# Values laid out feature by feature for the head mixing, and first-layer heads issued in pairs, in a two-layer gated transformer kernel on one core

## The reference, cut to what matters

```
# L0 attention: 16 heads of 64; ctx gives keys and values
q, k, v = query @ Wq.T, key @ Wk.T, value @ Wv.T       # 1024 columns = 16 heads x 64
weights = softmax(q @ k^T / 8 + padding mask + causal mask)   # per head, 256 x 256
out = (weights @ v) @ Wo.T + bo

# L0 feed-forward, first half: a small attention between the 16 heads of ONE token, HD = 16
q  = (h @ Wq + bq).reshape(b, t, H, HD)
kv = ((h @ Wdown + bdown) @ Wup + bup).reshape(b, t, H, 2 * HD)
k, v = split(kv, 2, axis=-1)
att = softmax(einsum('bthd,btgd->bthg', q, k) / 4)
out = einsum('bthg,btgd->bthd', att, v)
# ... then a mixture of 8 experts (We), gated per token
```

## Time and profile before

| what | value |
|---|---|
| median of three runs | 2798.7 us (2793.26 to 2803.64) |
| the profiled execution | 2801.4 us, its span 2799.6 us |
| busy over the span | PE 2515.2 us (90%), PEld 2056.0, DVE 1772.2 (63%), ACT 1268.1 (45%), POOL 958.5 (34%) |
| mean granted TensorE clock | 0.957 of full |
| first layer | from 0 to about 1490 us, 16 bodies with attention and two short ones behind |
| second layer | the rest, untouched by the change |

### The profile page before, as it was taken

How to read it: one execution, slowest core, us unless ns; L and a number is a source line. 1 busy time by engine, 2 the same in 40 slices (tenths; PEclk the granted TensorE clock), 3 DMA queues, 4 the chain that set the end, 5 groups by cost and what they waited for, 6 DMA issues and landing times. The chain is left out here.

```text
span 2799.6 us, 48038 instructions
## 1 busy us (share of the span) xinstructions
PE 2515.2 (90%) x16128; PEld 2056.0 (73%) x16128; DVE 1772.2 (63%) x3970; ACT 1268.1 (45%) x3939; POOL 958.5 (34%) x878
## 2 busy tenths in 40 slices
PE   6989999999999999999845699999999999999998
PEld 5767777777777777777635477777787777777877
DVE  3488888888788888888873544445444444444541
ACT  5644555445554456545402344444443433444441
POOL 1344544444444454443441223233222222232320
PEclk9999999999999999999956899999999999999999
DMA  4000000000000000000004000000000000000000
GB/s 138 13 5 16 13 4 15 15 15 12 4 15 15 15 12 4 15 15 8 5 4 153 8 9 13 15 15 15 15 15 15 15 15 4 11 15 15 15 8 8
DMA packets 25857, 51.67 MB, mean 18 GB/s; under 512 B 6272, under 2 KB 7040, under 8 KB 24640
## 3 DMA queue, kind: packets, MB, share of 16 engines
q1 hardware_dynamic: 25792, 50.84, 5.5%
HBM read 42.44 MB, written 8.39 MB: 18 GB/s over the span
## 5 line engine op out<-in xcount | busy, mean ns | idle before, releaser
L1147 POOL TENSOR_SCALAR l_probs<-l_probs,l_rinv 128x256 f32<-128x256 f32 x512 | 238.6, 481 | 589.9 <-DVE l_rinv L1362 588.3
L1258 ACT ACTIVATE l_probs<-l_score,l_negmax 128x256 f32<-128x256 f32 x512 | 238.9, 473 | 264.7 <-DVE l_negmax L1357 264.7
L1562 PE MATMUL l_ffn<-l_w,l_hid 128*128 128x256 f32 x1536 | 347.5, 381 | 1.0 <-ACT l_hid L1232 1.0
L318 POOL TENSOR_TENSOR l_prod<-l_q,l_kv 128x2048 f32<-128x2048 f32 x64 | 289.5, 4536 | 170.6 <-DVE l_att L580 92.7
L1562 PEld LDWEIGHTS l_ffn<-l_w,l_hid 128*128 128x128 f32 x1536 | 287.2, 190 | 50.5 <-issue 13.9
L332 POOL TENSOR_TENSOR l_prod<-l_att,l_kv 128x2048 f32<-128x2048 f32 x32 | 178.9, 5590 | 305.4 <-DVE l_att L597 178.1
L1369 DVE COPY l_probsT<-l_attn 128x512 f32<-128x512 f32 x256 | 175.6, 686 | 159.5 <-PE l_attn L1525 159.5
L677 DVE CUSTOM_DVE_ANT_0 l_probs<-l_score,l_mbias 128x256 f32<-128x256 f32 (+1 forms) x512 | 161.7, 353 | 118.5 <-PE l_score L872 91.2
L606 DVE TENSOR_TENSOR l_prod<-l_att,l_kv 128x2048 f32<-128x2048 f32 x32 | 217.6, 6799 | 3.4
L1357 DVE TENSOR_REDUCE l_negmax<-l_score 128x2 f32<-128x512 f32 x256 | 175.1, 684 | 65.5 <-PE l_score L1513 65.5
L404 ACT ACTIVATE l_probs<-l_probs,l_negmax 128x256 f32<-128x256 f32 x256 | 130.7, 511 | 186.5 <-DVE l_negmax L677 183.4
(11 more groups left out here) (267 smaller groups left out, 7510.1 us busy)
## 6 DMA issues: line engine op xcount, KB each, us to landing
l_ctxin<-in_ctx SPq DMA_DIRECT2D x32, 256.0 KB, 3.1
l_xin<-in_x SPq DMA_DIRECT2D x16, 256.0 KB, 2.7
l_x<-in_x SPq DMA_DIRECT2D x16, 256.0 KB, 2.6
x<-l_acc SPq DMA_DIRECT2D x16, 256.0 KB, 2.0
l_xin<-x SPq DMA_DIRECT2D x16, 256.0 KB, 3.2
l_x<-x SPq DMA_DIRECT2D x16, 256.0 KB, 2.7
out<-l_x SPq DMA_DIRECT2D x16, 256.0 KB, 2.0
l_hid<-in_w SPq DMA_DIRECT2D x2, 1536.0 KB, 8.8
```

The source lines that it names most:

```text
L318: nc.gpsimd.tensor_tensor(prod[:, u].rearrange("p (h g d) -> p h g d", h=half, g=H), q4[:, u * half:(u + 1) * half].unsqueeze(2).to_broadc ...
L1147: last = nc.gpsimd.tensor_scalar(probs[:, j % 4, t * S:(t + 1) * S], probs[:, j % 4, t * S:(t + 1) * S], rinv[:, j, t:t + 1], 1.0, ALU.mul ...
L1258: last = nc.scalar.activation(probs[:, s % 4, t * S:(t + 1) * S], ps[:, t * S:(t + 1) * S], ACT.Exp, bias=negmax[:, s, t:t + 1], accum_out ...
L1562: last = T.matmul(ps[:, 0:D], hid[:, c, t * P:(t + 1) * P], w2[:, c, :], start=c == 0, stop=c == 3 * NHC - 1)
```

## The change

There are two edits, both in the first layer.

1. The columns of the up projection's weights and bias are reordered on the host. Before, each of the 16 heads g had its 16 key columns and then its 16 value columns. Now all 256 key columns come first, head by head, and then the 256 value columns with the feature d outermost and the head g innermost. In the product att x v, where g is innermost, v was read with a step of 32 elements (128 bytes) and is now read with a step of one.
2. The heads of the first layer go in pairs. At each even step s both heads s and s+1 are scored, with the four matmuls alternating between the lower and the upper 64 partitions of the operands (rows of the array); at each odd step from 5 on two heads are multiplied with their values, alternating between the lower and upper 64 partitions of the output (columns of the array). `probsT` gets a third buffer, and to make room the tile `pos` is dropped: the mask bias is made in place, with one more drain on GpSimd. A pair waits for both score banks. For odd heads from 5 on `attn_max` also waits until head j-4 has been transposed.

```
-    pos, mbias = sb("pos", [P, S]), sb("mbias", [P, CAUSAL])
-    probs, probsT = sb("probs", [P, 4, CAUSAL]), sb("probsT", [P, 2, CAUSAL])
+    mbias = sb("mbias", [P, CAUSAL])
+    probs, probsT = sb("probs", [P, 4, CAUSAL]), sb("probsT", [P, 3, CAUSAL])
...
-    nc.gpsimd.tensor_scalar(pos[:], maskbits[:], -1.0, NEG, ALU.add, ALU.mult)
+    nc.gpsimd.tensor_scalar(mbias[:, 0:S], maskbits[:], -1.0, NEG, ALU.add, ALU.mult)
     pool.drain()
-    nc.gpsimd.tensor_tensor(mbias[:, 0:S], cmask[:, 0:S], pos[:], ALU.add)
-    nc.gpsimd.tensor_tensor(mbias[:, S:CAUSAL], cmask[:, S:CAUSAL], pos[:, 0:P], ALU.add).then_inc(mask_ready, 1)
+    nc.gpsimd.tensor_tensor(mbias[:, S:CAUSAL], cmask[:, S:CAUSAL], mbias[:, 0:P], ALU.add)
+    pool.drain()
+    nc.gpsimd.tensor_tensor(mbias[:, 0:S], cmask[:, 0:S], mbias[:, 0:S], ALU.add).then_inc(mask_ready, 1)
...
-    k4 = kv[:, t].rearrange("p (g two d) -> p g two d", two=2, d=HD)[:, :, 0, :]
+    k4 = kv[:, t, 0:D].rearrange("p (g d) -> p g d", d=HD)
...  # weigh (GpSimd, t = 0) and mix_weigh (VectorE, t = 1)
-    v4 = kv[:, 0].rearrange("p (g two d) -> p two d g", two=2, d=HD)[:, 1]
+    v4 = kv[:, 0, D:2 * D].rearrange("p (d g) -> p d g", d=HD)
...  # attn_copy (ScalarE)
-    if j >= 2:
-        act.wait_ge(pv_done, H * a + j - 1)
-    nc.scalar.copy(probsT[:, j % 2, :], ps[:, 0:CAUSAL]).then_inc(free, 1)
+    if j >= 3:
+        act.wait_ge(pv_done, H * a + j - 2)
+    nc.scalar.copy(probsT[:, j % 3, :], ps[:, 0:CAUSAL]).then_inc(free, 1)
...  # attn_max (VectorE)
+    if j >= 4 and j % 2 == 1:
+        _, transposed, _, when = attn.at(f"T{j - 4}", a)
+        wait_apart(dve, dve_passed, transposed, when)
...  # TensorE
+    def pair_scores(a, j):
+        c = j // HPC
+        ps0, full0, free0, turn0 = score.at(f"s{j}", a)
+        ps1, full1, free1, turn1 = score.at(f"s{j + 1}", a)
+        pe.wait_ge(free0, turn0)
+        pe.wait_ge(free1, turn1)
+        T.matmul(ps0[:, 0:S], qT[rows0, c, P:S], kT[rows0, c, :], start=True, stop=True)
+        T.matmul(ps1[:, 0:S], qT[rows1, c, P:S], kT[rows1, c, :], start=True, stop=True)
+        T.matmul(ps0[:, S:CAUSAL], qT[rows0, c, 0:P], kT[rows0, c, 0:P], start=True, stop=True).then_inc(full0, 1)
+        T.matmul(ps1[:, S:CAUSAL], qT[rows1, c, 0:P], kT[rows1, c, 0:P], start=True, stop=True).then_inc(full1, 1)
+    def pair_values(a, j):
...
+        both_emptied(pe, attn, f"T{j}", f"T{j + 1}", a)
+        T.matmul(ps[rows0, u * S:(u + 1) * S], v[:, 0, m0], p0[:, 0:S], start=True, stop=False)
+        T.matmul(ps[rows1, u * S:(u + 1) * S], v[:, 0, m1], p1[:, 0:S], start=True, stop=False)
+        T.matmul(ps[rows0, u * S + P:(u + 1) * S], v[:, 1, m0], p0[:, S:CAUSAL], start=False, stop=True).then_inc(pv_done, 1)
+        T.matmul(ps[rows1, u * S + P:(u + 1) * S], v[:, 1, m1], p1[:, S:CAUSAL], start=False, stop=True).then_inc(pv_done, 1)
...  # in body, step s
-    if a is not None and s < H:
+    if a is not None and s < H and s % 2 == 0:
...
-            head_scores(a, s)
+            pair_scores(a, s)
...
-            if s >= LAG_V:
-                head_values(a, s - LAG_V)
+            if s >= LAG_V0 and s % 2 == 1:
+                pair_values(a, s - LAG_V0)
```

More of the change, by code:

```diff
@@ L42 @@
 STEPS = H + LAG_V
-LAG_V1 = 5
+LAG_V0 = LAG_V1 = 5
 class Banks:
@@ L481, in body @@
                                 attn_copy(a, s - LAG_T)
-                            if s - LAG_V in (3, 7, 11):
-                                head_group(a, (s - LAG_V) // 4)
+                            if s in (7, 11, 15):
+                                head_group(a, (s - 7) // 4)
                             if s < H:
@@ L602, in mix_weigh @@
                 def mix_weigh(u):
-                    v4 = kv[:, 1].rearrange("p (g two d) -> p two d g", two=2, d=HD)[:, 1]
+                    v4 = kv[:, 1, D:2 * D].rearrange("p (d g) -> p d g", d=HD)
                     a4 = att[:, 1].rearrange("p (h g) -> p h g", g=H)[:, u * half:(u + 1) * half]
@@ L865, in moe_product @@
                     last.then_inc(full, 1)
-                def head_scores(a, j):
-                    c, r = j // HPC, slice((j % HPC) * HD0, (j % HPC + 1) * HD0)
-                    ps, full, free, turn = score.at(f"s{j}", a)
-                    pe.wait_ge(free, turn)
-                    T.matmul(ps[:, 0:S], qT[r, c, P:S], kT[r, c, :], start=True, stop=True)
-                    T.matmul(ps[:, S:CAUSAL], qT[r, c, 0:P], kT[r, c, 0:P], start=True, stop=True).then_inc(full, 1)
+                rows0, rows1 = slice(0, HD0), slice(HD0, P)
+                def pair_scores(a, j):
[8 more added lines that the diff above has]
+                    T.matmul(ps1[:, S:CAUSAL], qT[rows1, c, 0:P], kT[rows1, c, 0:P], start=True, stop=True).then_inc(full1, 1)
                 def head_transpose(a, j):
@@ L887, in head_values @@
                         pe.wait_ge(free, turn)
-                    attn.emptied(pe, f"T{j}", a)
-                    m = slice(j * HD0, (j + 1) * HD0)
-                    T.matmul(ps[r, u * S:(u + 1) * S], v[:, 0, m], probsT[:, j % 2, 0:S], start=True, stop=False)
-                    last = T.matmul(ps[r, u * S + P:(u + 1) * S], v[:, 1, m], probsT[:, j % 2, S:CAUSAL], start=False, stop=True)
-                    last.then_inc(pv_done, 1)
+                    both_emptied(pe, attn, f"T{j}", f"T{j + 1}", a)
+                    m0, m1 = slice(j * HD0, (j + 1) * HD0), slice((j + 1) * HD0, (j + 2) * HD0)
+                    p0, p1 = probsT[:, j % 3], probsT[:, (j + 1) % 3]
+                    T.matmul(ps[rows0, u * S:(u + 1) * S], v[:, 0, m0], p0[:, 0:S], start=True, stop=False)
+                    T.matmul(ps[rows1, u * S:(u + 1) * S], v[:, 0, m1], p1[:, 0:S], start=True, stop=False)
+                    T.matmul(ps[rows0, u * S + P:(u + 1) * S], v[:, 1, m0], p0[:, S:CAUSAL], start=False, stop=True).then_inc(pv_done, 1)
+                    T.matmul(ps[rows1, u * S + P:(u + 1) * S], v[:, 1, m1], p1[:, S:CAUSAL], start=False, stop=True).then_inc(pv_done, 1)
                 def attn_out(a):
@@ L968, in body @@
                                 head_transpose(a, s - LAG_T)
-                            if s >= LAG_V:
-                                if s - LAG_V == 8:
-                                    attn.emptied(pe, "v1", a)
-                                    attn.emptied(pe, "v3", a)
-                                head_values(a, s - LAG_V)
+                            if s >= LAG_V0 and s % 2 == 1:
+                                if s - LAG_V0 == 8:
+                                    for use in ("v1", "v3"):
+                                        _, _, emptied, turn = attn.at(use, a)
+                                        wait_apart(pe, pe_passed, emptied, turn + 1)
+                                pair_values(a, s - LAG_V0)
                             if s in own_at:
@@ L1660, in twice, with keys_then_values @@
         return np.concatenate([w, w], axis=-2).reshape(*w.shape[:-3], NC1 * P)
+    def keys_then_values(w):
+        w = w.reshape(*w.shape[:-1], H, 2, HD)
+        keys, values = w[..., 0, :], np.swapaxes(w[..., 1, :], -1, -2)
+        return np.concatenate([keys.reshape(*w.shape[:-3], D), values.reshape(*w.shape[:-3], D)], axis=-1)
     spread = np.zeros((H, SLOT, D), np.float32)
```

9 lines of the change are left out of this document (4 added, 5 removed).

## The result

The changed kernel takes 2712.6 us (median of four runs, 2710.55 to 2716.64) beside 2799.0 us for the kernel before on the same chip: 0.9694 of it, 95% interval 0.9673 to 0.9715. It is faster, as forecast, and in the range, but 33 us above the point of 2680: 88 us came off the profiled span (2799.6 to 2711.6) where 119 were forecast.

What follows compares the result with a forecast made beforehand. TensorE was taken to bound each 86.66 us body until step 15, then VectorE. Taking 7.2 us off 14 bodies (101 us), plus 7, 6 and 5 us elsewhere, gave 2680 us, range 2632 to 2722.

Steps and rivals of the forecast that it cites:

- its rival without them: Float32 pairs don't overlap on TensorE, so only the column reorder gains: 4.0 us per body, 2732 us; chance 0.07.
- The weighings: Both products of attention and values, GpSimd and VectorE: each ends 2.5 us sooner, 5.0 us in VectorE's tail.
- Until head 6: First, TensorE-bound stage of a body: VectorE gets head 6 1.5 us sooner; only 1.15 us passes the held gate operation.
- Steps 7 to 13: VectorE's waits for TensorE at steps 10 and 12 shrink from 2.00 to 0.9 and 0.73 to nothing: 1.8 us.
- The wait of odd heads costs nothing: Odd heads' wait for a transpose: hidden, as head j-4's transpose stands 1 to 6 us ahead of VectorE.
- TensorE last in the tail: Body's end: TensorE's attention output moves 5.75 us and finishes last; VectorE waits 0.9 us, next body starts 7.2 us sooner.
- The pairs overlap: Scores and values on TensorE: a pair takes one head's time, 13.1 us less TensorE work in a body.
- The rival "slower": TensorE's clock falls in each new gap, five for one: 1.8 us more per body, 2824 us; chance 0.05.

Runs made afterwards that it cites:

- edit 1 alone: The kernel before with only the value columns laid out feature by feature, no pairs: 2709.9 us, 0.9688 of the kernel before.
- filling the gap: The changed kernel with the values of heads 2 and 3 computed two more times ahead of the pair (8,9): 2710.0 us, 0.9684 of the kernel before.
- single scores: The changed kernel with each head scored on its own again, values still paired, no extra wait of odd heads: 2714.7 us, 0.9693 of the kernel before.
- the gate on ScalarE: The changed kernel with three small gate operations moved from VectorE to ScalarE as activations: 2671.0 us, 0.9538 of the kernel before.
- the tail filled: Last expert's product made three times, in the changed kernel with gate operations on ScalarE: 2680.1 us; with heads also scored singly: 2700.2 us.

## Why the prediction was right, and where it was too large

The range held, and in part by luck. What the forecast says of edit 1 on its two engines is right, and what it says of edit 2 is not: it gave the pairs 3.2 us of a body's 7.2 (its rival without them had 4.0), and beside edit 1 they are worth nothing (2712.6 and 2709.9 us). That the time still came out in the range is due to a second error the other way: edit 1 alone brings 5.7 us a body and not 4.0, because it also closes the gap behind which the clock fell in the tail, and no term of the sum has that.

- **The weighings (5.0 us).** Right, and shown by edit 1 alone. They gave 2.69 + 2.55 = 5.2 us. GpSimd takes 4.53 us (forecast 4.54), VectorE's product 2.15 us (forecast 2.29). The Trainium skill (GPSIMD Engine Reference, Performance pitfalls for Q7 kernels) would have had, as an estimate, 3.7 us by the ratio of its two prices; the trace does not agree: a step of one took 4.53 us where the step of 128 bytes took 5.6, a ratio of 0.81 and not 0.66.
- **Until head 6 (1.5 us for head 6, 1.15 for kv and through the gate).** Mis-sized: 0.08 and 0.43 in the body of the table, and later instead of sooner in those whose clock falls in step 5. TensorE's idle times came as forecast (1.11, 0.82 and 0.40 + 0.18 us against 1.1, 0.7, 0.7). What failed was to call the stage TensorE-bound because TensorE was busy 26.5 of 26.75 us. VectorE's list was just as tight: the low half of h2T is ready 21.2 us into the body in both kernels, the gate's product follows it at once (548.15 before; 518.14 after, waiting 0.18 us for it), and from there to head 6 TensorE has the transposes, one piece of values, q3 and the scores to do, 5.4 us in both, since the pair of values stands there in place of one head's. This is read from the two traces; no run takes VectorE's part away.
- **Steps 7 to 13 (1.8 us).** Failed: VectorE came to its first weighing 0.94 us later. Three things are in it. The held gate operation puts head 7 late and with it the pair (8,9): shown by the kernel that takes it away, -42 us. The fall of the clock behind the gap of 2.46 us, in half of the bodies, cost 1.0 us on the way to `xT_lo`: shown by filling the gap, though the clock then fell in the tail and the bodies stayed at 81.5 us. And the pair (10,11) waits for `attn_max` of head 9, so that the way to `xT_lo` stays 6.2 us and the wait 1.9 us however quick TensorE is: read from the trace of the filled kernel, not shown by a run of its own. The forecast had this coupling for the pair (8,9) and left it out for the pair (10,11).
- **"The wait of odd heads costs nothing".** Nearly: the gap in front of heads 7 and 9 grew from 0.24 to 0.43 us, and is 0.24 again where the wait is left out (single scores). 0.2 us, twice in a body.
- **TensorE last in the tail.** Half right. In 7 of the 14 bodies VectorE waits 1.7 us for the attention output, and the clock is low in the tail. In the other 7, and in all 14 of edit 1 alone, it doesn't: in the body of the table VectorE's sums end it (-4.77 us) with TensorE's output just ahead (-4.56, of which 2.3 us is the clock at 1.00: 14.7 us from head 15 to the end instead of 17.0, and 14.6 in edit 1 alone, without pairs). The sum took TensorE's wait for the sums as 1.54 us; in the bodies of the kernel before it is 1.5 to 2.8 us, and 2.75 at the start of the body that was read.
- **The pairs overlap.** Right: 0.85 us per pair, 12.1 us less work in a body. They were worth 14 us alone, nothing beside edit 1, and 38 us beside edit 1 and a free gate.
- **The rival "slower" (the clock falls in each new gap).** Its mechanism is real and its count was not: a body of the changed kernel has two falls, not five, and the mean granted clock of its 14 bodies is 0.95 (0.97 in the kernel before).

In short, the changed kernel stood on two bounds at once. Edit 1 alone brings the bodies to 81.0 us on the mean, where TensorE's 79.1 us of work nearly fill them; with the pairs TensorE has room, but VectorE with its held operation and its waits for TensorE needs 81.5. The best version here changes both, the gate on ScalarE with the pairs: 2671 us, 1.5% under the changed kernel.

Open: why the clock falls behind one gap and not behind another. In the changed kernel each gap of 2.5 us had a fall behind it, but that of 2.15 us had one in the body from 496.85 and none in that from 825.72; with single scores a gap of 3.4 us had none in 4 of 14 bodies; and the clock fell in step 5 of 7 of the 14 bodies behind gaps of 1.1 us and less. Open too is how the 38 us of the pairs are shared: the paired scores brought 20 us with the tail filled, and no run has single values with the gate on ScalarE and paired scores.

## What to carry to other kernels

An engine that is busy all through a stage need not be the only one that bounds it: check whether the engine it feeds, or is fed by, is ready at the same moment before crediting the stage with a saving. When work is grouped in pairs over two buffers, each pair waits for the newest of the two consumers, so every pair must be walked for this wait, not only the first that shows it. And a saving that becomes idle time on TensorE can take its clock down in the work behind it, so look at where the granted clock falls after the change, and at what waits there. Look at more than one body before you do: here neighbouring bodies of one execution differed by 3 us (80.3 and 83.3), with the clock low in different places.
